# Layernorm folded into Wk and Wv and into ACT's evictions; context loaded a chunk a slot

## What is computed

```python
a = (ctx - mean(ctx)) * rsqrt(var(ctx) + 1e-5) * gamma + beta      # per context row
Q = x @ Wq.T;  K = a @ Wk.T;  V = a @ Wv.T                          # 16 heads of 32
attn = softmax(where(mask, Q K^T / sqrt(32), -inf))
out  = x + tanh(gate) * (concat(attn V) @ Wo.T)
```

## Time and profile before

| what | value |
|---|---|
| three timed runs | 1026.55 us median (1025.28 to 1027.88) |
| profiled execution, its own time | 1022.71 us |
| its span (first to last instruction) | 1020.5 us |
| PE / DVE / ACT / POOL busy | 989.4 / 748.4 / 661.7 / 719.8 us |
| moved by DMA | 102.26 MB |
| mean granted PE clock | 0.987 of full |

### The profile page before, as it was taken

The page is one execution under the profiler, slowest core; times in us unless marked ns, Lnnn a source line. Parts: engine busy times, 40 slices in busy tenths (PEclk is TensorE's granted clock), DMA queues, the critical chain, the costliest instruction groups (busy, mean ns, idle before and its releaser), DMA issues.

```text
span 1020.5 us, 32130 instructions
## 1 busy us (share of the span) xinstructions
PE 989.4 (97%) x11665; PEld 831.9 (82%) x11665; DVE 748.4 (73%) x1414; ACT 661.7 (65%) x1364; POOL 719.8 (71%) x977
## 2 busy tenths in 40 slices
PE   9997999999999999999999999999999999999975
PEld 8896887888888888878888888888888888888863
DVE  6640388887877777787777787778887787877773
ACT  3313577766766766777666776667776676776662
POOL 1447878787777777787777787777878777775221
PEclk9999999999999999999999999999999999999997
DMA  9653433333334344433433443444333334331111
GB/s 298 195 160 68 124 93 83 88 100 105 81 104 106 101 109 107 108 88 88 103 85 96 110 105 102 109 107 110 85 95 102 90 89 112 82 81 30 31 36 41
DMA packets 83252, 102.26 MB, mean 100 GB/s; under 512 B 29024, under 2 KB 65888, under 8 KB 83200
## 3 DMA queue, kind: packets, MB, share of 16 engines
q10 hardware_dynamic: 24652, 56.60, 20.5%
q1 hardware_dynamic: 58548, 44.94, 17.1%
HBM read 91.34 MB, written 10.19 MB: 99 GB/s over the span
## 4 chain that ended last, share of the span: by engine, by line
PE 48%; DMA 26%; DVE 18%; issue 3%; POOL 1%; ACT 1%; SPq 1%; DVEq 0%; POOLq 0%; ACTq 0%
PE bank L766 33%; DMA row_max<-rmax 12%; DMA x<-row_max 10%; DVE rmax L714 7%; PE sbank L860 5%; PE bank L876 5%; DVE shared_f L724 4%; DVE bank L704 2%; DVE stats L673 2%; PE bank L782 2%; DVE top L701 1%; PE bank L885 1%; PE bank L881 1%; DMA row_stats<-row_stat 1%; PE sbank L782 1%
## 5 line engine op out<-in xcount | busy, mean ns | idle before, releaser
L766 PE MATMUL bank<-shared_r,w_k 128*128 128x376 f32 x1536 | 300.0, 344 | 5.8 <-ACT shared_f L622 5.7
L766 PE MATMUL bank<-w_v,shared_r 128*125 128x512 f32 x1152 | 284.8, 396 | 0.0
L766 PEld LDWEIGHTS bank<-shared_r,w_k 128*128 128x128 f32 x1536 | 259.6, 189 | 27.7 <-issue 21.1
L600 ACT ACTIVATE shared_f<-shared_f 125x448 f32<-125x448 f32 x384 | 201.4, 586 | 92.3 <-DVE shared_f L724 92.0
L766 PEld LDWEIGHTS bank<-w_v,shared_r 128*125 128x125 f32 x1152 | 213.3, 186 | 45.3
L714 DVE TRANSPOSE_TENSOR_REDUCE rmax<-shared_f 128x14 f32<-128x448 f32 x384 | 216.4, 614 | 36.5 <-ACT shared_f L569 36.4
L569 ACT ACTIVATE shared_f<-sbank,mask_b 125x448 f32<-125x448 f32 x384 | 215.7, 636 | 25.7 <-PE sbank L860 25.6
L724 DVE TENSOR_TENSOR shared_f<-shared_f,bank 125x448 f32<-125x448 f32 x384 | 215.4, 616 | 4.5
L452 POOL TENSOR_TENSOR shared_f<-shared_f 125x448 f32<-125x448 f32 x128 | 150.3, 1174 | 93.7 <-ACT shared_f L600 91.4
L413 POOL TENSOR_TENSOR cn<-cn,stat_bc 128x375 f32<-128x375 f32 x128 | 117.7, 952 | 91.3 <-DMA cn<-in_ctxT 76.8
L701 DVE TENSOR_REDUCE top<-x 128x14 f32<-128x168 f32 x128 | 55.9, 437 | 138.9 <-DMA x<-row_max 138.7
(11 more groups left out here) (65 smaller groups left out, 901.6 us busy)
## 6 DMA issues: line engine op xcount, KB each, us to landing
cn<-in_ctxT ACTq DMA_DIRECT2D x30, 750.0 KB, 6.0
rows<-in_ctx ACTq DMA_DIRECT2D x28, 720.0 KB
stat_bc<-row_stats ACTq DMA_DIRECT2D x29, 375.0 KB, 4.3
x<-row_max SPq DMA_DIRECT2D x128, 84.0 KB
xy<-in_x SPq DMA_DIRECT2D x32, 224.0 KB, 3.9
out<-xy SPq DMA_DIRECT2D x32, 224.0 KB
shared_f<-in_xT SPq DMA_DIRECT2D x7, 896.0 KB, 9.2
rows<-in_ctx SPq DMA_DIRECT2D x4, 720.0 KB
```

The lines of the kernel that those rows point to most:

```text
L600: act.activation(prob[0:SP_, (r - 3) % NB, j, :], prob[0:SP_, (r - 3) % NB, j, :], ACT.Exp, scale=SCALE).then_inc(exp_done, 1)
L766: last = pe.matmul(dst, l, m, start=(start and k == 0), stop=(stop and k == len(pairs) - 1))
```

## The change

- **Fold.** gamma is multiplied into Wk and Wv along the input dimension, and the mean over the input dimension is subtracted from each output column (`scaled_sum`, `mean`, `centre`). The mean needs a sum over partitions: a PE product with a matrix of 1/512. The row's mean of the context then drops out of K and V.
- **1/sqrt(var).** It becomes the `scale` of ACT's evictions of scores and of V (`rstd`, one value per context row, which is a partition there).
- **beta.** Its part in K is constant over the context rows, so softmax drops it. Its part in V becomes a constant row: beta through Wv (`bv`), that through Wo, times the gate (`gbo`), added to x by POOL (`add_bias`, one instruction per batch).
- **Removed.** `store_stats`, `load_stats`, `center`, `divide`, `affine`; POOL's row statistics have five steps and a last instruction instead of seven, one batch ahead instead of two.
- **Context.** Loaded by chunk (187.5 KB), one per slot, into eight chunk buffers; ACT issues. The rows are laid out `(j p)` instead of `(p j)`: 2 KB runs in place of 6 KB, so that `rstd` matches the partitions of K's and V's rows.
- **Query stage.** `q_group` runs bank by bank (m outside, k inside). New work is put between the groups on PE, and before, between and behind the splits on DVE, ACT and POOL; group loops are unrolled. The high and low parts of batch 0's context are made by DVE.

```diff
+            def products(dst, raw, factor, s_step, s_ready):      # POOL
+                for k in range(KT):
+                    to = dst if k == 0 else part
+                    if k > 1:
+                        pool.wait_ge(s_step, 2 * k - 1)
+                    pool.tensor_scalar(to[:, :], raw[:, k, :], factor[:, k:k + 1], None, ALU.mult) \
+                        .then_inc(s_step, 1)
+                    if k > 0:
+                        pool.wait_ge(s_step, 2 * k)
+                        pool.tensor_tensor(dst[:, :], dst[:, :], part[:, :], ALU.add) \
+                            .then_inc(s_step if k < KT - 1 else s_ready, 1)
...
+            pool.wait_ge(ld_const, 48)
+            pool.wait_ge(ld_w["v"], 16)
+            products(sum_b, raw_v, bet, mean_step, b_ready)
             row_statistics(0, 0)
             row_statistics(0, 1)
-            pool.wait_ge(ld_const, 48)
-            for c in range(2):
-                center(0, c, range(KT))
-                divide(0, c, range(KT))
-                affine(0, c, range(KT))
-            row_statistics(0, 2)
+            pool.wait_ge(bv_out, 1)
+            pool.wait_ge(mean_mm["k"], 1)
+            pool.wait_ge(ld_w["o"], 16)
+            products(gated, raw_o, bv, b_step, bo_ready)
...
+            x_group(1)                                             # DVE
             statistics(0, 0)
+            dve.wait_ge(ld_const, 48)
+            scaled_sum("k", raw_k, sum_k)
+            x_group(2)
+            scaled_sum("v", raw_v, sum_v)
+            x_group(3)
+            centre("k", raw_k)
+            weight_lo("k", raw_k, wk)
+            centre("v", raw_v)
+            x_group(4)
+            weight_lo("v", raw_v, wv)
+            x_group(5)
+            weight_lo("o", raw_o, wo)
             statistics(0, 1)
+            x_group(6)
+            x_group(7)
...
+            def centre(w, raw):
+                dve.wait_ge(mean_mm[w], 1)
+                if w == "v":
+                    dve.wait_ge(b_ready, 1)
+                for k in range(KT):
+                    dve.scalar_tensor_tensor(raw[:, k, :], raw[:, k, :], gam[:, k:k + 1],
+                                             mean_bank[w], ALU.mult, ALU.subtract) \
+                        .then_inc(centred[w], 1)
...
+            def beta_through_o():                                  # PE
+                pe.wait_ge(bo_ready, 1)
+                pe.wait_ge(q_out, 4 * KT)
+                pe.matmul(bo_bank[0:T, :], mean_w[:, 0:T], gated[:, :], start=True, stop=True) \
+                    .then_inc(bo_mm, 1)
...
             first_q_group()
+            q_group(1)
+            mean("k", sum_k, KT)
+            q_group(2)
+            mean("v", sum_v, 2 * KT)
+            beta_through_v()
+            q_group(3)
+            q_group(4)
+            beta_through_o()
+            for n in range(5, GROUPS):
+                q_group(n)
...
         def load_ctx(queue, i, m):
+            if behind(i, LOOP, m - 2 * KT + 1):
+                wait_apart(queue, c_done, i * LOOP + (m - 2 * KT + 1))
+            queue.dma_start(cn[:, m % (2 * KT), :], ctxT_v[i * 2 + m // KT, :, m % KT, :]) \
+                .then_inc(ld_ctx[m % (2 * KT)], 16)
...
+                                   bias=mask_b[0:SP_, c % 2, j:j + 1],
+                                   scale=rstd[0:SP_, c % 2, j:j + 1]).then_inc(s_out, 1)
```

More of the change, by code:

```diff
@@ L31, with xattn @@
 PASSES = ((0, 0), (0, 1), (1, 0))
-def xattn(nc, xT, x, ctx, ctxT, mask, wqT, wkT, wvT, woT, gamma, beta, gate, out, row_stats):
+def xattn(nc, xT, x, ctx, ctxT, mask, wqT, wkT, wvT, woT, gamma, beta, gate, out, row_max):
     es = ExitStack()
@@ L134, in xattn @@
         spread = bank[MB][:, 0:HT]
+        sum_k, sum_v, sum_b, part = gated, xy[:, 0, :], xy[:, 1, :], gbo
+        mean_bank = {"k": bank[3], "v": bank[7]}
+        bv_bank, bo_bank = bank[6][:, 0:KT], bank[7]
         ld_const = sem("ld_const")
@@ L503, in _ @@
             pool.wait_ge(q_out, GROUPS * KT)
+            pool.wait_ge(c_done, KT)
             slots(pool, slot)
@@ L623, in slot @@
                         .then_inc(k_done, 1)
-                if not early(i, r):
+                if live(i, LOOP, r + 6, SLOTS) and behind(i, LOOP, r + 3):
                     context_hi(i, r)
@@ L688, in _, with scaled_sum @@
[L688 to L696 removed]
+                                      ALU.subtract).then_inc(w_done[w], 1)
+            def scaled_sum(w, raw, dst):
+                dve.wait_ge(ld_w[w], 16)
+                dve.tensor_scalar(dst[:, :], raw[:, 0, :], gam[:, 0:1], None, ALU.mult) \
+                    .then_inc(sum_ready[w], 1)
+                for k in range(1, KT):
+                    dve.wait_ge(sum_ready[w], k)
+                    dve.scalar_tensor_tensor(dst[:, :], raw[:, k, :], gam[:, k:k + 1], dst[:, :],
+                                             ALU.mult, ALU.add).then_inc(sum_ready[w], 1)
@@ L756, in slot @@
                                       ALU.subtract).then_inc(o_done, 1)
-                if u == 1 and live(i, 2, c + 4, B) and behind(i, 2, c + 2):
-                    statistics(i, c + 4)
+                if u == 1 and live(i, 2, c + 2, B) and not first_two(i, c + 2):
+                    statistics(i, c + 2)
             slots(dve, slot)
@@ L785, in q_pass, with mean, beta_through_v @@
                                  stop=(k == KT - 1 and e == len(PASSES) - 1))
+            def mean(w, total, behind_q):
+                pe.wait_ge(sum_ready[w], KT)
+                pe.wait_ge(q_out, behind_q)
+                pe.matmul(mean_bank[w], mean_w[:, :], total[:, :], start=True, stop=True) \
+                    .then_inc(mean_mm[w], 1)
+            def beta_through_v():
+                pe.wait_ge(b_ready, 1)
+                for m in range(KT):
+                    last = pe.matmul(bv_bank[:, m:m + 1], sum_b[:, 128 * m:128 * m + 128],
+                                     ones[:, 0:1], start=True, stop=True)
+                last.then_inc(bv_mm, 1)
+            def beta_through_o():
[3 more added lines that the diff above has]
+                    .then_inc(bo_mm, 1)
             def first_q_group():
```

290 lines of the change are left out of this document (134 added, 156 removed).

## The result

The changed kernel takes **1029.82 us** in the median (1028.09 to 1030.81, 16 runs), the kernel before 1024.47 us (1021.14 to 1031.58, 16 runs). The ratio is 1.0048 [1.0031, 1.0065]: slower by 5.35 us, 0.5%. That lies within the predicted range of 1023 to 1034 and 1.8 us above the predicted 1028.0. The likeliest case, no difference that can be told (0.50), did not come; "slower" had a chance of 0.37. That the time itself is so near is in part luck: the predicted 1028.0 stood on three runs of the kernel before whose median was 2.1 us higher than that of 16, and the difference was forecast as 1.5 us and came out as 5.35.

A forecast was written before the change was run, and what follows sets the result against it. PE's own work was taken as the bound, with losses only in irregular slots and at the start. Start +5.2 and slots -2.9 gave +2.3 us profiled (1025.0); timed, +1.5 on 1026.55 gave 1028.0, range 1023 to 1034.

The forecast's parts named there:

- The likeliest case, no difference that can be told: Whole kernel: time within 0.3% (3.1 us) of the kernel before; chance 0.50.
- The mechanism at the fold: Query stage, behind group 4: PE waits for POOL's products of beta with Wo, ready at 70.2 us; stall 10.8 us.
- Contention with `x_group(6)`: Query stage: DVE's split beside POOL's products lengthens them from 7.7 to 10.0 us, by 2.3.
- Group 3 ends: Query stage: PE finishes group 3 at 49.7 us, after the means, the beta products and a short wait for DVE.
- The lower bound from K and V rows: Query stage: the mean's two 512-column records take at least 0.5 us, judged by K and V products; 1.3 taken.
- the warm-up products: Query stage: 128-column products of 0.48 us, times four 1.92, as upper measure for a mean's product; 1.3 taken.
- The wait for `centre` of k: Query stage, last bank of group 2: PE waits 0.5 us (0 to 2) for DVE's centred Wk.
- Behind the stall: Query stage after the fold: product 1.3 us, groups 5 to 7 29.2, lower clock 2.3; first K at 103.0.
- Lead-in: First K to first scores: the 5.75 us stall for ACT goes, scores follow 10.6 us after first K; start +5.2.
- The rival in which the stall stays: Lead-in: another wait replaces ACT's, first scores come 8 us later, 1036 us; chance 0.05.
- Slots: Slot loop: exchanges meet less context load, 12.8 us falls to about 10, irregular slots vanish; -2.9 us.
- the exchange is not relieved: Rival for the slot loop: smaller, constant loads still slow exchanges, none of the 2.9 us returns; 1031.8 us, chance 0.31.

The follow-up runs named there:

- two_op_k_outer: Changed kernel with a second operation (adding 0.0) in GpSimd's scaling and query groups 4, 6, 7 with k outside, m inside; 1029.46 us in one run.
- kept_busy: Changed kernel with 60 PE products that nobody reads ahead of the wait for the fold's operand; 1026.99 us.
- burst: Changed kernel with ACT issuing a batch's four context chunks together instead of one per slot; 1029.42 us.
- few_stats: Kernel before, with ACT's broadcast load of statistics cut from 375 KB to 8 KB from batch 3 on; 1021.39 us, ratio 0.9969.
- burst_extra: burst plus an unread 187.5 KB broadcast load per batch, issued ahead of the four chunks; 1030.87 us, ratio to the kernel before 1.0057.
- before_x_first: Kernel before, with SP loading query groups 4 and 5 ahead of the store and broadcast load of batch 0's statistics; 1023.51 us, ratio 0.9975.
- changed_again: The changed kernel run once more, unedited; 1030.09 us, ratio to the kernel before 1.0037.

## Why the prediction was right or wrong

**The mechanism at the fold: right, its sizes too low.** The chain was as told: end of group 3, `x_group(5)`, rest of Wo, statistics of batch 1, row statistics, seven products. From 51.06 to 74.55 us it took 23.5 instead of 20.5. The split took 3.3 (3.1 with 0.3 of hand-overs), Wo 2.4 (2.5), the statistics 2.3 (2.2). The row statistics took 3.1 (2.4), and the products 12.3 (10.0). **The mis-sized term is GpSimd's scaling**: I scaled the `affine` rows by size, to 0.9 us a scaling, but `affine` has two operations and `products` one, and that form takes 1.56. `two_op_k_outer` shows it. Contention with `x_group(6)` I had put at 2.3; it is 3.41 - 1.56 = 1.85 in the first scaling and 0.99 - 0.20 = 0.79 in the last row statistic, 2.6 in sum. So the terms were 2.6 too low for four scalings (4 x 0.66) and 0.3 for contention, and the rest is small. The stall was 13.6 us instead of 10.8.

**Group 3 ends at 51.06 instead of 49.7.** The mean for k cost 27.34 - 26.88 = 0.46 us where I took 1.3, that for v 40.45 - 39.59 = 0.86 (1.3), the beta products 0.81 (0.7). The lower bound from K and V rows was the right end for k, the warm-up products the wrong measure. The wait for `centre` of k went the other way: 1.89 us, with what drains before it 2.4, where I took 0.5 with a bound of 2. DVE's scaled sum of v (first instruction 0.92 instead of 0.49 us) and its split of group 3 (2.18 and 2.40 instead of 1.09 and 2.03) run beside POOL's first `products`. I counted POOL's contention only on `centre`, and had group 3 split at 31.2 where it was at 34.2. Together with a start 0.4 later this is +1.4.

**Behind the stall: right.** The product 1.06 (1.3), group 5 11.27, groups 6 and 7 9.92 each: 31.1 us where I had 29.2 + 2.3 = 31.5. `kept_busy` shows the clock as the cause: at full clock the product and group 5 are 1.6 us shorter, so the 2.3 was a little high. The 0.4 in groups 6 and 7 is the execution's. First K came at 106.7, not 103.0.

**Lead-in: right.** No wait takes the place of ACT's; 10.45 us to the scores, 10.6 predicted. The rival in which the stall stays is out. The start was thus +8.8 instead of +5.2: 1.4 ahead of the fold, 3.0 in it, and 0.8 given back.

**Slots: size right for the profiled execution, reason wrong in two points.** The stretch fell by 2.93 us, I had 2.9. The whole surplus of the profiled execution went, as forecast; but that surplus differs by 7.8 us between two executions of the slots of before, so its size fitted this pair only. I gave as reason that the exchange meets 187.5 KB of context instead of 1125 KB. `burst` sends all four pieces together and the stretch is the same; `few_stats` leaves the 750 KB load alone and cuts the broadcast of the statistics, and DVE's waits for the exchange fall from 138.7 to 18.3 us. Of the 1125 KB it is the 375 of the broadcast that made the exchange late. How it does so is open: half of it (`burst_extra`) did little, and whether its bytes or its form count was not tried. The rival "the exchange is not relieved" did not come true, though its 1031.8 lies near the result; the missing 3.6 us were at the start. The second point is POOL. It is 465 us busy (I had 440) and so 254 less, and I gave that no worth in the slots, because no row of the profiled execution had PE wait for POOL. Two other executions have such rows, 1.39 us in `few_stats` and 2.29 in `before_x_first`, where a late context load held `center` and `center` held the sum behind it. In `few_stats` these waits stand in both slots that make up its surplus. So a part of what the slots gain may come from POOL's shorter program; how large it is in the timed runs no experiment shows, for none shortens it alone.

**What I costed at nothing.** The per-row scale on ACT is 87 ns an eviction, not nothing; in the slots it is covered, in the drain it is 0.3 us. The added addition on POOL "has time", but it slows DVE by 0.9 us at the one place where DVE's rest is on the path. That is the collision which I had taken from the Trainium skill, GPSIMD Engine Reference, Key points, for `products` and had not looked for here. With the output projection behind the gaps there (4.94 us in this execution, 4.21 in that of before, 3.86 in that of `changed_again`) the end was 0.3 + 0.9 + 0.7 = +1.9 where I had 0; 1.2 of it is the change's.

**From the profile to the timed runs.** The profiled executions differ by 1030.07 - 1022.71 = 7.36 us, where I had 2.3. The median of before lies 1.76 above its profiled one (1024.47 by 16 runs; I had 3.8 by three), that of the changed kernel 0.25 below: 7.36 - 1.76 - 0.25 = 5.35. So the difference of the profiles was 5.1 us larger than forecast and the timed one 3.9. That the timed runs of before hold more such stalls than the profiled one fits: before spreads over 10 us and the changed kernel over 3, and the slow execution of `before_x_first` shows the long exchanges. Open is why before's median moved between 1024.1 and 1032.0 us from series to series. The changed kernel had 1029.8 and 1030.1 us, beside 1024.5 and 1026.1 of before; it was never run beside the 1032.0, so whether it would have moved there is not shown.

## What to carry to other kernels

When work is folded into a preparation stage, write down for the one operand on which the bound engine waits everything that stands ahead of it in program order on each engine, and move what it does not need behind it: two calls exchanged on an engine that had stood idle for 17 us gave 17 us here. Size an instruction by a row of the same form, the number of its operations included, and not only of the same shape. Where a stall comes and goes between executions, look at which small round trip runs beside a broadcast load, and try that load alone before crediting the bytes. An engine whose wait appears in no row of one execution can still hold the bound engine in another: look at what stands in its program ahead of the operand, and at more than one execution.

## What the runs showed of the hardware

- GpSimd's `tensor_scalar` on 128x512 fp32 with a factor from memory takes 1.56 us with one operation and 0.69 with a second one (`+ 0.0`).
- ACT's eviction of 125x448 from PSUM takes 636 ns with a constant scale and 723 with one from memory.
- A GpSimd operation beside a DVE operation with two inputs slows one of them or both: DVE's 128x448 rest 0.58 to 1.50 us, its three-instruction scaled sum 2.63 to 3.85 (2.32 alone), GpSimd's 128x512 addition 1.26 to 2.04, its one-operation scaling 1.56 to 3.41. Beside a DVE cast of 1.09 us a GpSimd step of 0.20 us took 0.99.
- The write and read of 21 KB through HBM took 7.20 + 6.83 us in one exchange beside the loads of before; without the broadcast, DVE's waits for such reads fell from 138.7 to 18.3 us.
- After 13.6 us without work PE's granted clock was 0.50 for about 3 us; with 60 products that nobody reads in the gap it was 1.00 at once, and the two-record product and the 48 behind it were 1.6 us shorter.
- The same 48 products take 9.73 or 9.92 us from start to start, at a granted clock of 1.00 in both cases; in the first execution of the changed kernel the groups behind the stall are the long ones, in `changed_again` they are the short ones (9.73) and those ahead of it the long ones (10.0 for group 3). Why is open.
